# The value pieces of the first slot stand behind the turn of the maxima, with two fillers in their place

## The reference

```python
x = x + xattn(_layernorm(x), ctx, Wq, bq, Wk, bk, Wv, bv, Wo, bo)
x = x + ffn(_layernorm(x), ...)
# xattn, 16 heads of 16 channels
q = Wq @ x + bq; k = Wk @ c + bk; v = Wv @ c + bv
scores = einsum('bhkt,bhks->bhts', q, k) * SCALE
p = softmax(scores); out = einsum('bhts,bhks->bhkt', p, v)
return Wo @ out + bo
# ffn: rmsnorm, router over 8 experts with the best 2, silu(g) * u, w_down, and a shared expert
```

## Time and profile before

| | |
|---|---|
| median of three runs | 850.28 us |
| the profiled execution | 849.69 us, its span 847.9 us |
| TensorE busy | 95% of the span |
| VectorE, ScalarE, GpSimd busy | 61%, 47%, 42% |
| mean granted TensorE clock | 0.996 |

### The profile page before, as it was taken

How to read it: one execution, slowest core, us unless ns; L and a number is a source line. 1 busy time by engine, 2 the same in 40 slices (tenths; PEclk the granted TensorE clock), 3 DMA queues, 4 the chain that set the end, 5 groups by cost and what they waited for, 6 DMA issues and landing times. The chain is left out here.

```text
span 847.9 us, 11463 instructions
## 1 busy us (share of the span) xinstructions
PE 803.9 (95%) x3771; PEld 388.6 (46%) x3771; DVE 518.1 (61%) x1043; ACT 401.1 (47%) x751; POOL 353.1 (42%) x288
## 2 busy tenths in 40 slices
PE   6999999999999999999999998999999999999993
PEld 2434434444444444444433454443555555555552
DVE  5787888787777877878788655568542222222221
ACT  1115666767677677676776663110422323333231
POOL 4207417326354274253220211000117777777774
PEclk9999999999999999999999999999999999999998
DMA  8957557646665566466633223931626555655553
GB/s 275 211 95 224 114 127 166 132 103 141 145 137 129 119 157 149 103 149 143 131 80 106 91 77 110 415 111 51 251 56 99 98 97 97 101 90 96 95 98 43
DMA packets 54956, 110.48 MB, mean 130 GB/s; under 512 B 12580, under 2 KB 27684, under 8 KB 50660
## 3 DMA queue, kind: packets, MB, share of 16 engines
q1 hardware_dynamic: 37852, 80.23, 37.5%
q0 software_dynamic: 16960, 29.37, 18.4%
q10 hardware_dynamic: 88, 0.16, 0.1%
HBM read 68.44 MB, written 41.16 MB: 129 GB/s over the span
## 5 line engine op out<-in xcount | busy, mean ns | idle before, releaser
L963 DVE TENSOR_REDUCE negmax<-front_ps 128x1 f32<-128x512 f32 x512 | 323.6, 681 | 85.9 <-PE front_ps L816 85.5
L725 ACT ACTIVATE probs<-st_ps 128x512 f32<-128x512 f32 x512 | 280.2, 601 | 166.6 <-PE st_ps L850 149.9
L1215 POOL DMA_INDIRECT out<-x_sb,row_i x78 | 122.0, 1564 | 70.3 <-ACT x_sb L1263 57.0
L1408 PE MATMUL big_ps<-w_gu,attn 128*128 x312 | 140.4, 593 | 0.8 <-ACT attn L1255 0.8
L1602 DVE TENSOR_TENSOR zeros<-attn,big_ps 128x256 f32<-128x256 f32 x39 | 16.4, 421 | 116.3 <-ACT attn L1275 116.3
L850 PE MATMUL st_ps<-stacks 50*128 50x512 f32 x256 | 77.7, 488 | 5.4 <-ACT probs L725 4.3
L1408 PEld LDWEIGHTS big_ps<-w_gu,attn 128*128 128x128 f32 x312 | 56.2, 190 | 57.0 <-issue 57.0
L410 POOL TENSOR_TENSOR attn<-attn,recip 128x512 f32<-128x512 f32 x15 | 19.2, 1278 | 150.1 <-DMA recip<-rec_dram 150.1
L850 PE MATMUL st_ps<-q_stack,k_stack 50*128 50x512 f32 x256 | 74.6, 491 | 3.9 <-ACT probs L725 2.8
L580 POOL CAST early<-early 128x512 fp32r<-128x512 f32 x28 | 17.1, 610 | 136.4 <-ACT early L678 136.4
L816 PE MATMUL front_ps<-stacks 48*128 48x512 f32 x256 | 68.7, 434 | 3.8 <-DVE negmax L963 3.0
(11 more groups left out here) (199 smaller groups left out, 1056.6 us busy)
## 6 DMA issues: line engine op xcount, KB each, us to landing
parts_dram<-early SPq DMA_DIRECT2D x32, 512.0 KB, 6.2
stacks<-parts_dram SPq DMA_DIRECT2D x32, 256.0 KB, 5.6
w_gu<-in_gate_up SPq DMA_DIRECT2D x8, 1024.0 KB, 13.4
x_sb<-in_x SPq DMA_DIRECT2D x8, 512.0 KB, 9.9
early<-in_ctx POOLq DMA_DIRECT2D x8, 512.0 KB, 7.1
stacks<-parts_dram SPq DMA_DIRECT2D x32, 128.0 KB, 5.9
k_stack<-parts_dram SPq DMA_DIRECT2D x16, 256.0 KB, 5.1
q_stack<-parts_dram SPq DMA_DIRECT2D x16, 256.0 KB, 5.6
```

The costliest lines, as they stand in the source:

```text
L725: nc.scalar.activation(probs[:, k % 2, u % GH, :], score_bank(UNITS * s + u), ACT.Exp, scale=SCALE).then_inc(exp_done, 1)
L963: nc.vector.tensor_reduce(negmax[:, n % 2, c:c + 1], smax_bank(UNITS * n + u), AX_X, ALU.max, negate=True).then_inc(max_done, 1)
L1215: nc.gpsimd.indirect_dma_start(outs[i], bass.IndirectOffsetOnAxis(ap=row_i[:, k:k + 1], axis=0), y_sb[:, k % RING, DY * i:DY * (i + 1)], N ...
L1408: mm = nc.tensor.matmul(gu_ps[:, :], h_t[:, k % 2, a, :], w_gu[:, bass.ds(expert, 1), a, :], start=(a == 0), stop=(a == DT - 1))
```

## The change

The turn of slot 0 moves from u = 16 to u = 14. The two value pieces of slot 0 move from u = 10 and 14 to u = 18 and 26, as in the other slots; ScalarE's copies follow them to 20 and 28, and VectorE's parts of the maxima come at u = 16. The first piece now waits for those parts, the turn no longer for the pieces' copies, and fillers of 384 columns into `proj_ps` stand at u = 10 and 12, behind the wait for the eighth projected half.

```diff
         def turn_unit(s):
 
-            return 16 if s == 0 else 12
+            return 14 if s == 0 else 12
 
         def late_units(s):
 
-            return (10, 14) if s == 0 else (18, 26)
+            return (18, 26)
@@ project_v
                     if r == 1:
                         pe.wait_ge(vt_copied, 2 * b + 1)
-                    elif b < 2:
-                        pe.wait_ge(qk32_ready, 4 * (b + 1))
+                    elif b == 0:
+                        pe.wait_ge(qk32_ready, 4)
                     else:
                         pe.wait_ge(nm_parts_ready, turns(2 * b - 1))
@@ turn_max
-                    pe.wait_ge(vt_copied, values_before(max(n - 1, 1)))
+                    pe.wait_ge(vt_copied, values_before(n - 1))
@@ the slots
                         if s == 0 and u == 0:
                             filler(pv_ps[:, :])
+                        if s == 0 and u in (10, 12):
+                            pe.wait_ge(qk32_ready, 2 * (FIRST + 1))
+                            filler(proj_ps[:, 0:FILL])
```

## The result

The changed kernel takes 853.49 us (median of 8 runs, 853.11 to 855.1), the kernel before it 850.5 in the same comparison. The ratio is 1.0033 with a 95% interval of 1.002 to 1.0045: slower by 3.0 us. That is inside what I counted as no change (0.5%), but the interval lies above 1, so the slowdown itself is clear of the scatter. The forecast was 852.1, the range 849.9 to 854.2. The profiled execution has a span of 851.4 against 847.9, 3.5 us more; the profiled one before the change was 0.8 us under the median of its runs, so the traces show more of a difference than the medians do.

A forecast was written before the change was run, and what follows sets the result against it. TensorE, busy 95% of the span, was taken as the bound. Terms of -0.58, +1.40 and +1.32 summed to +2.1 us, giving 851.8 or 852.4; 852.1 was taken, eight in ten between 849.9 and 854.2.

The forecast's parts named there:

- The wait at the turn: Slot 0, unit 14: TensorE waits for the last maxima from 75.12 to about 77.0, some 1.9 us.
- The working's sum: End of slot 0: -0.58 at unit 18, +1.40 and +1.32 for the two value pieces, +2.1 us.
- unit 18 to 22: Slot 0's cycle with the first value piece: 4.26 us, 4.56 with some 0.3 of wait for the parts; cost 1.40.
- the second piece's cycle: Slot 0, from unit 26: 4.26 us with the value piece, a cost of 1.32.
- a piece's cover: Slot 2's cycles with and without a piece: 0.61 us of a piece lies in waits that were there anyway.
- The clock: Rival: TensorE falls to 1.2 GHz after its 1.9 us wait, +4 us on top, 856; chance 0.04.
- my own signs: Wrong if the turn's gap is under 1 us, slot 0's lag is gone by slot 3, or the stretch's clock is below 1.00.
- pieces without cover: Rival, slot 0's pieces: both cost 1.93, or the parts' wait is longer by as much; +3.3, 853.3; chance 0.09.
- Given back later: Rival, after slot 0: the 2.1 us delay ends at a wait that keeps its own time; 849.7 to 850.3; chance 0.11.
- Short wait: Rival, the turn: maxima come at 75.64, unit 16's scores start 1.2 us sooner; +0.9, 850.9; chance 0.13.
- The turn meets finished maxima: Rival: passes spread ahead of the turn make its wait nil; +0.2, 850.3; chance 0.03.
- What was priced at nothing: Rows and stacks leaving some 2.2 us earlier, GpSimd's later split of value weights, the turn's dropped wait: no effect.

The follow-up runs named there:

- filled: The changed kernel with two more fillers (512 and 384 columns) in front of the turn at unit 14; 852.03 us, ratio 1.0018.
- half filled wait: The changed kernel with one more filler of 512 columns in front of the turn at unit 14; 852.07 us, ratio 1.0025.

## Why the prediction was right, and where it fell short

**The order of the work came out as added up.** Times from unit 8 on, mine and the changed kernel's: unit 12 3.98 (3.97), the `pv` of unit 12 5.00 (5.04), unit 14 6.85 (6.88), unit 16 9.85 (9.89). The wait at the turn: some 1.9 forecast, 1.84 in the brackets. The working's sum, +2.14, has its direct test in the two kernels with a filled or half filled wait: +2.21 each, and to the scores of unit 30, where the last cycle of the sum ends, +2.13 and +2.12. Single terms, from the filled one: unit 16 to 18 1.67 (78.53 - 76.87 = 1.66); unit 18 to 22 4.56 (83.07 - 78.53 = 4.54), with 0.21 of wait for the parts where I had 0.3 (my own figures, 79.8 - 79.56, give 0.24); the second piece's cycle 4.26 (90.26 - 86.01 = 4.25). Reading a piece's cover from slot 2 was the step that made this good.

**The clock is the term that was missing.** I gave it 0.04 and a price of 4 us; it happened and cost 1.3. The trace shows it for the profiled execution. For the other runs only the mean clock speaks: 3.4 us at half clock take 0.002 off it (an estimate, 3.4 x 0.5 / 850), and all 8 runs of the changed kernel have 0.990 to 0.993, where 8 of the 12 runs with the wait filled have 0.994 to 0.996. The mean clock alone proves no fall at the turn, since 13 of 35 runs of the kernel before have 0.991 to 0.993 too, and a fall at 517 us like the one above gives such a mean. By my own signs the prediction was wrong in this ("if the clock of this stretch is below 1.00"). That 853.49 still lies in the range is luck as far as the clock goes: the highest rival inside it was that of pieces without cover (853.3), and the clock's own forecast, 856, lay outside. The failed step is the argument from the earlier trace rows: that TensorE had nothing to do from 836 and the clock was still 1.00 until 840, so 1.9 us could not matter. In the changed kernel the fall comes not in the wait but 1.2 us after its end and 3.0 after its start, with TensorE busy again. A row that shows how late a fall comes says nothing of how short a gap is enough. The Trainium skill (TensorE: Matmul & The Clock Gate, "What's actually happening") says that the throttled state is the default and that activity releases the throttle. By that rule the clock was at risk, and the trace of the changed kernel agrees: 1.00 until 77.5, 0.50 from 78 to 81.25. The price was too high since I let it last through a whole cycle and doubled its waits too.

**The rivals.** Given back later: no, the lag is 3.22 at slot 1 and 3.30 at 515. Short wait: no, 1.84. No cover: no, the cycles are 4.54 and 4.25. The turn meets finished maxima: no.

**What was priced at nothing was nothing.** The rows of the maxima left at 79.56 instead of 82.05, with no effect; the load of these rows started at 83.36 for 83.54, so of the 2.5 us only 0.2 reached even the next transfer. GpSimd's split of the value weights moved to 90.13, and its next item, at 99.45, waited for ScalarE as before.

What stays open: why the clock falls in some executions of one kernel and not in others, and where it falls in the long runs without slot 1's fillers.

## What to carry to other kernels

A wait that is moved costs itself and what it does to the clock. Where an engine works in a fixed order, put the waiting instruction behind the work that covers it; if it must wait, multiply zeros meanwhile, which here gave back 1.3 us and took nothing, with one filler as with two. A filler or a moved piece costs its length less the waits that the cycle had anyway; read that cover from a place in the same kernel where such a piece already stands. Compare traces by the distance between two marks around the change, not by absolute times or medians that differ by less than the runs scatter. A low mean clock says that the clock fell somewhere in an execution, not where, nor that it cost anything.

## What the runs showed of the hardware

The granted clock fell to 1.2 GHz after a wait of 1.84 us, but late: the matmuls of the first microsecond after the wait still ran at 2.4 GHz, and the half rate then lasted 3.4 us although TensorE was busy all the time. It did not fall after a wait of 0.79. After a gap of 0.98 at 516.75 it fell in one profiled execution, from 517.4 to 520.75, and not in the one before the change, at 0.97; that fall cost nothing, since a wait of 1.12 for VectorE stood behind it. It fell once with no single gap of note, in the kernel with the turn at 16 and without fillers, from 72.1 to 75.5, behind short scores and passes held by VectorE. In the kernel with slot 1's fillers left out, the same code took 849.1 or 858.4 us at mean clocks of 0.995 and 0.98.
